# Layer 0 attention: the product with V moved two steps behind its scores, evacuation and value copy one step later

## What is computed

```
x = x + L0_xattn(layernorm(x), ctx, ctx, mask)     # <- the change is in here
x = x + L0_ffn(layernorm(x))                       # router, 8 experts
x = x + L1_xattn(layernorm(x), ctx, ctx, bias)     # 2 x 16 x 512 x 1024 scores
x = x + L1_ffn(layernorm(x))                       # 8 experts, top 2

# L0_xattn
scores = einsum('bhqd,bhkd->bhqk', Q, K) / sqrt(16)
scores = where(mask, -inf, scores)                 # mask[0, 0, q, k], for all heads
attn_w = softmax(scores, axis=-1); attn_w = where(isnan(attn_w), 0, attn_w)
out    = einsum('bhqk,bhkd->bhqd', attn_w, V) @ Wo.T + bo
```

## Time and profile before

| | |
|---|---|
| median of 3 runs | 1120.2 us (1116.76 to 1128.48) |
| profiled execution, its own time | 1119.18 us |
| its span | 1117.5 us |
| TensorE matmul busy | 1061.6 us (95% of the span) |
| VectorE / ScalarE / GpSimd busy | 547.0 / 467.9 / 478.2 us |
| layer 0 attention loop | about 77 to 274 us of the span |

### The profile page before, as it was taken

How to read it: one execution, slowest core, us unless ns; L and a number is a source line. 1 busy time by engine, 2 the same in 40 slices (tenths; PEclk the granted TensorE clock), 3 DMA queues, 4 the chain that set the end, 5 groups by cost and what they waited for, 6 DMA issues and landing times. The chain is left out here.

```text
span 1117.5 us, 25242 instructions
## 1 busy us (share of the span) xinstructions
PE 1061.6 (95%) x10041; PEld 784.8 (70%) x10041; DVE 547.0 (49%) x1534; ACT 467.9 (42%) x738; POOL 478.2 (43%) x507
## 2 busy tenths in 40 slices
PE   7899999999899999999998999999985999999997
PEld 4555555544578888888774358765455999999997
DVE  5579888864831111111248988888454211122121
ACT  4367666666531111111052688888843111111110
POOL 5358888882056780000013445455403233323232
PEclk9899999999999999999989999999996999999999
DMA  8635222002546955447058422200017999999970
GB/s 225 171 94 99 45 45 46 2 3 86 199 160 183 350 186 185 146 145 219 6 160 221 87 49 59 59 16 2 2 39 228 377 379 340 314 313 318 301 249 2
DMA packets 90434, 170.72 MB, mean 153 GB/s; under 512 B 11862, under 2 KB 62248, under 8 KB 87888
## 3 DMA queue, kind: packets, MB, share of 16 engines
q1 hardware_dynamic: 81720, 157.56, 45.1%
q0 software_dynamic: 6048, 8.28, 3.1%
q10 hardware_dynamic: 2560, 3.41, 1.1%
HBM read 150.19 MB, written 19.54 MB: 152 GB/s over the span
## 5 line engine op out<-in xcount | busy, mean ns | idle before, releaser
L1543 ACT ACTIVATE prob<-st_ps 128x1024 f32<-128x1024 f32 x186 | 189.5, 1022 | 58.5 <-PE st_ps L198 54.3
L198 PE MATMUL s_ps<-k_stack,q_stack 97*32 97x512 bf16 x1904 | 209.5, 381 | 3.2 <-DVE mx L265 2.3
L198 PE MATMUL st_ps<-q_stack,k_stack 100*32 100x512 bf16 x2048 | 192.5, 379 | 2.0 <-ACTq L1510 0.9
L265 DVE CUSTOM_DVE_ANT_0 junk<-s_ps,bias_rows,mx 128x512 f32<-128x512 f32 x240 | 169.9, 748 | 24.2 <-PE s_ps L198 24.2
L265 DVE CUSTOM_DVE_ANT_0 junk<-s_ps,bias_rows 128x512 f32<-128x512 f32 x236 | 154.6, 689 | 38.4 <-PE s_ps L198 38.4
L1992 PE MATMUL h_ps<-expert_in,w 128*128 (+1 forms) x704 | 153.5, 379 | 2.0 <-DMA w<-in_w 1.3
L1423 PE MATMUL o_ps<-prob,v_unit 128*32 128x512 f32 x1024 | 143.5, 595 | 5.1 <-POOL prob L1335 3.4
L1992 PEld LDWEIGHTS h_ps<-expert_in,w 128*128 128x128 f32 (+1 forms) x704 | 131.4, 187 | 22.6 <-issue 2.7
L1335 POOL TENSOR_TENSOR prob<-prob,keep_cols 128x1024 int32<-128x1024 int32 x56 | 132.8, 2381 | 18.7 <-ACT prob L1543 18.4
L198 PEld LDWEIGHTS st_ps<-q_stack,k_stack 100*32 100x32 bf16 x2048 | 81.3, 97 | 67.3 <-issue 21.8
L198 PEld LDWEIGHTS s_ps<-k_stack,q_stack 97*32 97x32 bf16 x1904 | 76.1, 95 | 70.0 <-DVE mx L265 37.8
(11 more groups left out here) (360 smaller groups left out, 1443.7 us busy)
## 6 DMA issues: line engine op xcount, KB each, us to landing
wg<-in_gateT SPq DMA_DIRECT2D x23, 1024.0 KB
wu<-in_upT SPq DMA_DIRECT2D x23, 1024.0 KB
wd<-in_downT SPq DMA_DIRECT2D x23, 1024.0 KB
w<-in_w SPq DMA_DIRECT2D x16, 1368.0 KB
w<-in_w SPq DMA_DIRECT2D x8, 1280.0 KB
k_stack<-k_scr SPq DMA_DIRECT2D x16, 384.0 KB, 5.1
k_stack<-k_scr SPq DMA_DIRECT2D x16, 256.0 KB, 5.6
k_scr<-k_parts SPq DMA_DIRECT2D x24, 128.0 KB, 2.9
```

Of the source, the lines that this page charges most:

```text
L198: mm = pe.matmul(out[cols], weights[:, cols], moving, start=start, stop=stop)
L265: self.pr.nc.vector.tensor_tensor_reduce(out=self.junk[:, self.bank("job", u, j)], in0=self.ps[:, self.bank("job", u, j)], in1=self.m.bias ...
L1543: nc.scalar.activation(prob[:, n % 2, 2 * hp:2 * hp + 2], st_ps[:, 2 * hp:2 * hp + 2], ACT.Exp).then_inc(exp_done, 1)
```

## The change

In layer 0, `weigh` of step n - 2 stands in step n behind the scores of head 1 and the one row job after them, where `weigh` of step n - 1 stood at the end of step n; the last two are issued after the last step. `evacuate(u - 1)` on ScalarE stands behind the exponentials of the unit's second step in place of its first, and `values(u + 1)` on GpSimd behind the second keep in place of the first. Layer 1 keeps its order. No instruction is added or removed, and no buffer.

```diff
@@ gpsimd
-                            if kt == 0:
+                            if kt == 1:
                                 values(u + 1, *divmod(u + 1, B))
@@ tensor, step(u, kt), l == 0, in the loop over h
                             if h:
                                 row.scores(pe, jobs[h - 1:h])
+                            if h == 1 and u * KT + kt >= 2:
+                                weigh(*divmod(u * KT + kt - 2, KT))
@@ tensor, end of step
-                    if kt or u:
+                    if l == 1 and (kt or u):
                         weigh(*divmod(u * KT + kt - 1, KT))
                     row.scores(pe, jobs[3:])
@@ tensor, after all steps
+                if l == 0:
+                    weigh(NU - 1, KT - 2)
                 weigh(NU - 1, KT - 1)
@@ scalar
-                        if kt == 0 and u:
+                        if kt == 1 - l and u:
                             evacuate(u - 1)
```

## The result

The changed kernel takes 1133.06 us (median of 10 runs, 1131.71 to 1143.22), the kernel before 1123.24 us in the same measurement (10 runs, 1116.76 to 1128.84). The ratio is 1.0114, with a 95% interval of 1.0088 to 1.0141: about 1.1% slower. The two medians are 9.8 us apart; the ratio stands for 12.8 us, its interval for 9.9 to 15.8. The profiled execution has a span of 1130.8 us, 13.3 us more than before's, where +13.6 was forecast.

The account below looks back on a forecast made before the run. TensorE, busy 95% of the span and full in the loop, was taken as the bound; +0.8 +4.7 +2.5 -1.1 +0.5 +6.2 = +13.6 us on 1119.2 gave 1132.8, plus 1.0 to the median, stated as 1134, range 1125 to 1140.

Parts of the forecast that it names:

- (f): Unit 0, five row jobs a step: the gap between jobs leaves VectorE idle some 0.15 us a step; +0.8 us.
- (c): Units' first weigh stalls 0.93 us behind the later evacuation of the same bank; +4.7 us over five units.
- (d): Row ring, steps 3 and 6: the job behind a turn comes about 0.25 us late, ten times; +2.5 us.
- (e): Units 2 and 4: longer lead, idle time and evacuation stall cover GpSimd's late keep, removing 0.54 us each; -1.1 us.
- (g): Unit 6's last three steps, without row jobs: cycle of weigh, exponentials, next head 0 takes 2.65 us; +0.5 us.
- (h): Unit 7: mask add waits for a weigh in its step, 2.87 us cycle, plus 1.7 us evacuation stall; +6.2 us.
- (a): Plain steps: exponentials of heads 0 and 1 move behind the weigh, with 0.17 us of cover; costs nothing.
- Rival 3: Plain steps: the exponentials' cover is missing, heads wait some 0.1 us in 40 steps, +4; 1139 us, chance 0.17.
- Rival 1: TensorE catches up stalls by starting groups closer than 0.217 us; only latency chains cost, +5.6, 1126 us; chance 0.12.
- Rival 2: Not slower: evacuation gets before the weigh, longer lead removes TensorE's 3.4 us keep waits; 1117 to 1120 us, chance 0.08.

Follow-up runs that it names:

- e4: Changed kernel with the weigh 0.22 us earlier in its step, in front of the first row job; ratio to the kernel before 1.0146.
- e6: Kernel before with only the evacuation and the value copy one step later, the weigh in its old place; ratio 1.0096.
- e8: Changed kernel with VectorE's layer 0 row maxima taken over 384 of each 512 keys; ratio to the kernel before 1.0084.
- e1: Changed kernel with the evacuation behind the exponentials of a unit's first step again; ratio to the kernel before 1.0109.
- e7: Kernel before with GpSimd's value copy behind the seventh keep of a unit, nothing else; ratio 1.0008.
- e9: Kernel before with the value copy behind the seventh keep in units 0 to 5 only, unit 6 as it was; ratio 0.9981.
- e2: Changed kernel with unit 7 in the old order, its weigh and last evacuation back by a step; ratio to the kernel before 1.0076.
- e3: Changed kernel with the weigh 0.65 us later in its step, behind head 2 and the second row job; ratio to the kernel before 1.0412.

## Why the prediction was right

It was right in sign and place, and in the loop's size. The time of 1134 us forecast against 1133.06 owes something to chance: it stood on a median of three runs before, 1120.2, which came out at 1123.24, while the medians moved apart by 9.8 and not by 13.6 us. The profiled executions, 1119.18 and 1132.77 us, are 13.6 apart. The loop's +13.2 us by its steps:

| step of the prediction | predicted | measured |
|---|---|---|
| (f) unit 0 | +0.8 | 27.70 against 26.86 us from head 0 of step 0 to head 0 of step 8: +0.84 |
| (c), (d), (e) units 1 to 5 | +4.7 + 2.5 - 1.1 = +6.1 | 129.92 against 124.47 us from weigh to weigh: +5.45 |
| (g) unit 6 to head 0 of step 57 | +0.5 | 262.39 - 234.63 = 27.76 against 27.22: +0.54 |
| (h) unit 7 | +6.2 | 285.47 - 262.39 = 23.08 against 16.70: +6.4 |

(a) Plain steps take 3.04 us as before, so the exponentials' cover was there; e4 shows that more of it is worth nothing. Uncovered, the ring of weigh, exponentials and next scores is seen in unit 6, where two of the steps without row jobs are 2.63 and 2.64 us apart (2.65 predicted). Rival 3 is out.

(c) The wait was 0.90 us where 0.93 was predicted, but two errors cancel in that, which is luck: the evacuation started 0.2 us earlier (3.75 after head 0, not 3.95), and from its end at 112.09 to the weight load at 112.31 there were 0.22 us, not 0.05. These 0.22 us stand in all six units and in e4, e6 and e8 alike. The first weigh of unit 7, which has no keep to wait for, has its load 0.07 us after the evacuation (267.30 to 267.37). The other six wait for four semaphores and this one for three; whether that makes the difference was not tried. e1 moves this wait by moving the evacuation alone, and e6 makes one of 1.80 us with the weigh in its old place.

(d) The job behind a turn came 0.18 us late in step 3 and 0.24 in step 6 (3.40 and 3.46 against 3.22, two a unit), where I took 0.25. e8 shows that it is VectorE's maximum that is waited for. This is 0.4 of the 0.65 us by which units 1 to 5 were over-predicted, and (c) most of the rest.

(e) The waits for keep went, and the reason given needs its last clause: not the longer lead but "the stall of (c)" covered them. e1, without the stall, has them again. (The weigh's old place is 158.82 - 153.82 = 5.00 us, where the prediction has 4.98; nothing hangs on it.)

(f) The +0.84 is one execution's: unit 0, counted between the same two head scores, differs by 0.5 us between e7 and e9, which have the same order there. And VectorE is not all that paces it: two of its steps wait for GpSimd (e8), which the prediction did not have.

(h) A ring of 2.90 us (2.87 predicted) and one wait of 1.67 us (1.7), and e2 takes both away.

Rival 1, stalls caught up: behind the wait at 112.34 the next groups start 0.86 and then 0.22 us on, as always, and nothing is made good. TensorE's weight loads are busy for 11.15 us in unit 1 after and were for 14.06 before, with 386 loads in both. The load time fell by a fifth with the same loads, and at 57% of unit 1 before it left nothing to spare. Perfetto Trace Analysis (section Identifying the Most-Contended Engine) in the Trainium skill names the share of weight loads as a measure of TensorE's headroom, with the share of peak FLOP/s beside it. This case's trace does not bear out the first; the second was not worked out. Rival 2 is out with (c).

## What to carry to other kernels

Count the distance between a producer, the engine that empties its buffer and the next writer in time and not in steps: two moves by one step each shrank it here, because the weigh also moved forward within its step. When work is moved in a loop whose bound engine is full, write down each ring through it (here weigh, exponentials, next scores; weigh, mask add, next scores; weigh, both exponentials, head 2) with its own length, and do so again for the stretches where the cover is thinner, the last unit above all: it held almost half of the loss. A wait that disappears in the profile may only be hidden under a new one.

## What the runs showed of the hardware

In e6 TensorE had no matmul for 2.65 us before the weigh at 273.18 in unit 7, and the granted clock from 273.2 to 276.8 us was 0.53 of full speed, close to the lower level of 1.2 GHz:

```profile
271.00:273.20 2.20, 0.02 (x4) 0.05 (x5) 0.00 (x0) 2.08 (x3) 1.52 (x1) 1.00 0.85 310
273.20:276.80 3.60, 3.60 (x29) 1.62 (x33) 0.96 (x1) 0.00 (x0) 1.14 (x1) 0.53 0.03 9
276.80:280.00 3.20, 3.20 (x48) 1.20 (x44) 1.49 (x2) 2.39 (x3) 0.00 (x0) 1.00 0.00 0
```

```profile
273.18 1.77 PE L1423 MATMUL o_ps<-prob,v_unit 128*32 128x512 f32 x8 [2.65 <-ACT prob L1560]
274.65 1.58 PE L198 MATMUL st_ps<-q_stack,k_stack 100*32 100x512 bf16 x12
```

That weigh took 1.77 us in place of 1.07, and the next one came after 3.84 us in place of 2.34: 1.5 us more on top of the wait. In the changed kernel the idle time at the same place was 1.50 us, and the clock stayed at 1.00 after it.

That the idle time brought the clock down is likely but not shown. It is the only fall in the loop from 86 us on in any of the eleven profiles. But in e3, e6, e7 and e9 the clock also fell to 0.50 between 74 and 78 us, in front of the loop, where TensorE had not been idle for more than 0.35 us at a time from 66 us on; in the other seven it stayed at 1.00 over the same work. Where such a stretch reaches into the loop, as in e3 and e6, the loop is longer for another reason than the edit.
